# Many-head cross-attention: half of the bundles masked on GpSimd in SBUF, where matmuls masked them in PSUM

## The chip, the cores and the metric

The program runs on one core of one Trainium2 chip, in one launch. It is a whole network of twelve layers, each a stage of its own. The metric is the device time of the program in microseconds, the median over runs. Engines go by the profile's names: PE is TensorE (PEld its weight loads), DVE is VectorE, ACT is ScalarE, POOL is GpSimd, SP is SyncE, which issues the loads.

## The reference

Only the seventh layer is touched, `_L2_xattn_ref`: cross-attention with 16 heads of 8 dimensions, from 64 queries to 1601 keys, for each of 32 batch elements. The mask is the same for all elements and heads.

```python
def _L2_xattn_ref(query, key, value, mask, W_q, W_k, W_v, W_o):
    Q = _split(query @ W_q.T)          # (32, 16, 64, 8)
    K = _split(key @ W_k.T)            # (32, 16, 1601, 8); key = value = ctx_1024
    V = _split(value @ W_v.T)
    scores = jnp.einsum('bhqd,bhkd->bhqk', Q, K) / jnp.sqrt(jnp.float32(D_K))
    scores = jnp.where(mask, -jnp.inf, scores)
    attn_w = jax.nn.softmax(scores, axis=-1)
    attn_w = jnp.nan_to_num(attn_w, nan=0.0)
    out = jnp.einsum('bhqk,bhkd->bhqd', attn_w, V)
    ...
    return merged @ W_o.T
```

`query` is the layernorm of x, and the result is added to x.

## The kernel before

`many_head_cross_attention` (from line 2458) is one stage with five engine programs that meet at semaphores. Everything is in fp32, except for a few bf16 constants. The order of each engine's work is written out by hand over a common counter b, one step for one bundle.

**Bundles.** The keys of an element are cut into 13 chunks of 128 (the last has 65). A bundle is two chunks of keys by half of the heads (two groups of four, `gi` 0 and 1, which sit in two row groups of 32 of TensorE). Seven pairs of chunks (`step` 0 to 6, the last a single chunk) times two halves (`half` 0, even, and 1, odd) make `ROUND` = 14 bundles for an element and 448 in all.

**Steps of TensorE** at b, in order:
- `less_max(b)` writes minus the row's maximum into the score banks `st` (three, in turn, one for each `gi`; it waits until the exponentials have read the bank).
- `query_by_keys(b + LEAD)` makes scores in the other orientation, 18 bundles ahead, for the maxima (three banks `mx`).
- `no_bounds(b)`, line 2610, for even bundles only: up to eight bf16 matmuls which add 2 x -2^100 (`bounds`, made of the mask) to the masked scores through one-hot columns (`places_b`), so that their exponential is 0.
- `keys_by_query(b)`, line 2621, adds keys times queries.
- `values(b - 2)`, line 2670, multiplies the exponentials of an earlier bundle with the values and adds them up in the bank `pv`. For an even bundle it waits for the exponentials (`exped`), for an odd one for VectorE's cap (`capped`). The first bundle of an element is done three behind.
- `prepare`: one unit of a later element's transposes (T), values (V) or keys (K), through the bank `prep`, or of the ends (M, E1 to E3).

**The others.** ScalarE takes the exponential of both halves of a bundle into `pT[b % 5]` in SBUF (lines 2846 and 2849; it waits until the values of the bundle five back are done) and copies the prepared units. VectorE does the masked maxima of bundle b + 18 (line 2765: one pass each, scores in PSUM plus the mask in SBUF), and for odd bundles the cap, line 2811: a tensor_tensor minimum of the exponentials with `capT`, which is 0 for a masked key and 2 for an open one. An open exponential is near or below 1, so it passes. It also copies `pv` out and does the ends of an element. GpSimd has one instruction per element, the spread of the queries into `qb` (line 2583), which waits until the scores three elements back are done. SyncE loads weights, constants, the mask in several layouts and then the keys of each element.

Of the kernel before, what the change touches and what calls it, by code (L numbers as in the profile page):

```python
# [2457 lines left out]
def many_head_cross_attention(c, name):  # L2458
# [9 lines left out]
    with Stage(c, name) as s:  # L2468
# [14 lines left out]
        pT = [s.sb(f"pT{u}", [P, 2, 2, 256]) for u in range(5)]  # L2483
# [24 lines left out]
        capped = s.sem("capped")  # L2508
# [63 lines left out]
        def _(pool):  # L2572
# [4 lines left out]
            pool.wait_ge(loaded, 304)  # L2577
            for n in range(B):
                if n == 0:
                    pool.wait_ge(*V.at("q3"))  # L2580
# [4 lines left out]

        @block.tensor
        def _(pe):
# [3 lines left out]
            pe.wait_ge(loaded, 304)  # L2591
# [10 lines left out]

            def no_bounds(b, n, step, half, i, c2):

                j = 2 * step + c2
                if j >= KC:
                    return
                for gi in (0, 1):
                    w, r = 2 * b + gi, 32 * (2 * half + gi)
                    nc.tensor.matmul(st[0:chunk[j], w % 3, 256 * c2:256 * c2 + 256], bounds[i][r:r + 32, P * j:P * j + chunk[j]],  # L2610
                                     places_b[i][r:r + 32, :, :].rearrange("p h q -> p (h q)"), start=False, stop=False,
                                     tile_position=(r, 0))
# [40 lines left out]
            def values(b):  # L2653
# [4 lines left out]
                else:  # L2658
                    pe.wait_ge(exped, 2 * b + 2)
# [76 lines left out]
        def _(dve):  # L2736
            dve.wait_ge(loaded, 304)
# [60 lines left out]
            for b in range(FIRST, LAST):  # L2798
# [14 lines left out]
                n, off = divmod(b - ROUND - 1, ROUND)  # L2813
# [376 lines left out]
```

## Time and profile before

| what | value |
|---|---|
| median of 3 runs | 3734.1 us (3729.46 to 3734.45) |
| profiled execution, its time | 3733.86 us |
| its span | 3732.0 us, mean granted TensorE clock 0.848 |
| busy over the span | TensorE 2816.8 us (75%), VectorE 2138.5 (57%), ScalarE 1409.1 (38%), GpSimd 425.2 (11%) |
| this stage | from about 1173 to 2515 us of the span; its bundles from about 1288 to 2511 |

Busy times are those of each engine by itself, and an engine that waits isn't busy. Matmuls are pipelined and their ends are modelled, so that starts of instructions tell more than busy shares of TensorE. A row of the timeline has the start in us from the start of the span, the duration, engine, line, operation, output and inputs with their shapes, how many of them in a row, and in brackets how long the engine was idle before and what ended it. A mean in a group is in ns.

### The profile page before, as it was taken

Reading aid. Unit: us, or ns where it says so; the run is one execution under the profiler, and the core shown is the slowest. Engines: PE = TensorE matmul, PEld = TensorE weight load, DVE = VectorE, ACT = ScalarE, POOL = GpSimd, SP = SyncE. Lnnn points to the kernel's source line nnn. Section 1 sums busy time; section 2 is a strip of 40 time slices with the busy share of each in tenths; the row PEclk is TensorE's granted clock in tenths of the full one; section 3 lists DMA queues with packets and bytes.
Section 4 is the critical chain, followed back from the end, with each engine's and each line's share of the span. In section 5 each row is a group of like instructions: output and inputs, shape, how many; then the busy total and the mean of one; then the engine's idle time right before and its main releaser. Section 6 shows DMA issues by size and latency. Waiting matters only on the chain. (4 is left out here: it accounts for less than half of the span.)

```text
span 3732.0 us, 67368 instructions
## 1 busy us (share of the span) xinstructions
PE 2816.8 (75%) x27776; PEld 1805.1 (48%) x27806; DVE 2138.5 (57%) x6291; ACT 1409.1 (38%) x2463; POOL 425.2 (11%) x275
## 2 busy tenths in 40 slices
PE   7866743696986999999999999993544557887723
PEld 4655532464664466666666666651211224565412
DVE  4432312574112377777777777745999853444776
ACT  3431211463332255555555555533211122443521
POOL 2310011340000000000000000000445400001300
PEclk9995776797998599999999999976777767898956
DMA  7740032000001001010000101001122100552000
GB/s 168 176 104 0 14 96 50 7 3 13 18 18 29 27 20 28 20 28 20 28 20 20 28 20 28 2 6 50 68 112 90 45 12 9 134 133 53 8 0 11
DMA packets 207265, 160.11 MB, mean 43 GB/s; under 512 B 12194, under 2 KB 195717, under 8 KB 202832
## 3 DMA queue, kind: packets, MB, share of 16 engines
q1 hardware_dynamic: 205936, 153.95, 15.0%
q8 instruction: 221, 3.62, 0.4%
q0 software_dynamic: 1024, 1.85, 0.2%
q14 instruction: 84, 0.69, 0.1%
HBM read 151.57 MB, written 4.46 MB: 42 GB/s over the span
## 5 line engine op out<-in xcount | busy, mean ns | idle before, releaser
L2765 DVE CUSTOM_DVE_ANT_0 L_xattn_junk<-L_xattn_ps_mx,L_xattn_shift 128x512 f32<-128x512 f32 (+1 forms) x1024 | 545.0, 569 | 360.0 <-issue 358.9
L2846 ACT ACTIVATE L_xattn_pT<-L_xattn_ps_st 128x512 f32<-128x512 f32 x768 | 416.8, 595 | 421.1 <-PE L_xattn_ps_st L2621 421.1
L2634 PE MATMUL L_xattn_ps_mx<-L_xattn_kT,L_xattn_qb 32*128 32x512 f32 (+1 forms) x2048 | 501.8, 568 | 0.4 <-ACT L_xattn_kT L2861 0.4
L2621 PE MATMUL L_xattn_ps_st<-L_xattn_qb,L_xattn_kT 32*128 32x256 f32 (+1 forms) x3328 | 447.3, 383 | 0.0
L2621 PEld LDWEIGHTS L_xattn_ps_st<-L_xattn_qb,L_xattn_kT 32*128 32x128 f32 (+1 forms) x3328 | 297.0, 185 | 24.6
L2811 DVE TENSOR_TENSOR L_xattn_pT<-L_xattn_pT,L_xattn_capT 128x512 f32<-128x512 f32 (+1 forms) x448 | 271.4, 647 | 37.3 <-ACT L_xattn_pT L2846 32.4
L2670 PE MATMUL L_xattn_ps_pv<-L_xattn_pT,L_xattn_v 128*17 128x128 f32 x6656 | 268.0, 280 | 0.0
L2670 PEld LDWEIGHTS L_xattn_ps_pv<-L_xattn_pT,L_xattn_v 128*17 128x17 f32 x6656 | 148.0, 98 | 162.6 <-issue 161.1
L2634 PEld LDWEIGHTS L_xattn_ps_mx<-L_xattn_kT,L_xattn_qb 32*128 32x128 f32 x2048 | 161.7, 188 | 8.8 <-DVE L_xattn_tops L2765 6.1
L2044 ACT ACTIVATE L_attn_da<-L_attn_dt,L_attn_na 128x2016 f32<-128x2016 f32 x32 | 63.2, 1976 | 270.2 <-DVE L_attn_db L2003 140.2
L1785 DVE SCALAR_TENSOR_TENSOR x<-L_ffn_ps_o,L_ffn_weights,x 128x128 f32<-128x128 f32 x128 | 36.1, 345 | 224.5 <-PE L_ffn_ps_o L1698 224.5
L2583 POOL TENSOR_TENSOR L_xattn_qb<-ln_sq,L_xattn_four 128x256 f32<-128x256 f32 x32 | 19.5, 612 | 1198.3 <-PE L_xattn_ps_st L2621 1170.8
L447 PE MATMUL L_xattn_ps_turn<-ident,L_xattn_ctx 128*128 128x128 f32 (+1 forms) x832 | 126.3, 289 | 39.1 <-ACT L_xattn_ctxT L564 28.2
L2647 PE MATMUL L_xattn_ps_st<-L_xattn_less,L_xattn_ones_b 3*128 3x512 bf16 x768 | 154.8, 391 | 1.1 <-ACT L_xattn_pT L2846 1.1
L1932 PE MATMUL L_attn_ps_all<-L_attn_db,ident 128*128 128x512 f32 x128 | 84.4, 820 | 87.5 <-POOL L_attn_db L1955 87.5
L1816 ACT ACTIVATE L_ffn_gelu<-L_ffn_ps_h,L_ffn_b1e 128x512 f32<-128x512 f32 x128 | 87.8, 687 | 163.4 <-PE L_ffn_ps_h L1691 160.1
L1698 PE MATMUL L_ffn_ps_o<-L_ffn_w,L_ffn_gelu 128*128 128x128 f32 x1024 | 122.8, 278 | 24.9 <-ACT L_ffn_gelu L1816 24.9
L1698 PEld LDWEIGHTS L_ffn_ps_o<-L_ffn_w,L_ffn_gelu 128*128 128x128 f32 x1024 | 116.7, 192 | 51.4 <-ACT L_ffn_gelu L1816 51.4
L2692 PE MATMUL L_xattn_ps_prep<-L_xattn_wv,L_xattn_ctxT 128*128 128x128 f32 (+1 forms) x832 | 132.0, 300 | 2.3 <-ACT L_xattn_v L2864 2.0
L2610 PE MATMUL L_xattn_ps_st<-L_xattn_place_b,L_xattn_bounds 32*128 32x256 bf16 (+1 forms) x1664 | 131.1, 272 | 0.0
L2696 PE MATMUL L_xattn_ps_prep<-L_xattn_ctxT,L_xattn_wk 128*128 128x512 f32 (+1 forms) x256 | 128.2, 584 | 2.4 <-ACT L_xattn_kT L2861 2.0
L447 PEld LDWEIGHTS L_xattn_ps_turn<-ident,L_xattn_ctx 128*128 128x128 f32 (+1 forms) x832 | 95.1, 146 | 68.1 <-issue 24.8
(552 smaller groups left out, 5472.2 us busy)
## 6 DMA issues: line engine op xcount, KB each, us to landing
L_xattn_ctx<-in_ctx SPq DMA_DIRECT2D x96, 768.0 KB
L_attn_bb<-scratch_rows SPq DMA_DIRECT2D x16, 1024.0 KB, 4.8
L_attn_cc<-scratch_rows SPq DMA_DIRECT2D x16, 1024.0 KB, 6.9
L_xattn_mask<-in_mask_keys SPq DMA_DIRECT2D x32, 400.2 KB, 6.9
L_ffn_w<-in_L_ffn_w SPq DMA_DIRECT2D x32, 256.0 KB, 3.1
L_ffn_w<-in_L_ffn_W SPq DMA_DIRECT2D x16, 256.0 KB, 3.0
L_xattn_mask<-in_mask_pairs SPq DMA_DIRECT2D x32, 100.1 KB, 4.5
L_xattn_ctx<-in_ctx SPq DMA_DIRECT2D x96, 32.5 KB
```

Source lines behind the costliest of these rows:

```text
L447: last = nc.tensor.transpose(tp[g % 2][:, P * (j % 4):P * (j % 4) + k], ctx[0:k, u, b, j, :], c.ident[0:k, 0:k])
L1698: last = nc.tensor.matmul(po[:, i % 2, P * j:P * j + P], g[:, i % 2, k, P * j:P * j + P], w2[:, u, k, :], start=(k == 0), stop=(k == FC - 1))
L2610: nc.tensor.matmul(st[0:chunk[j], w % 3, 256 * c2:256 * c2 + 256], bounds[i][r:r + 32, P * j:P * j + chunk[j]], places_b[i][r:r + 32, :, : ...
L2621: last = nc.tensor.matmul(st[0:chunk[j], w % 3, 256 * c2:256 * c2 + 256], kT[n % 3][r:r + 32, P * j:P * j + chunk[j]], qb[n % 3][r:r + 32, ...
L2634: last = nc.tensor.matmul(mx[:, w % 3, to:to + width], qb[n % 3][32 * g:32 * g + 32, 2 * (p % 2):2 * (p % 2) + 2, :].rearrange("p h q -> p ...
L2647: nc.tensor.matmul(st[:, w % 3, :], ones_b[r:r + 3, :], less[n % 2][r:r + 3, :, :].rearrange("p c k -> p (c k)"), start=True, stop=False, ...
L2670: last = nc.tensor.matmul(pv[32 * q:32 * q + 17, P * half:P * half + P], v[n % 3][0:chunk[j], j, 4 * half + q, :], pT[b % 5][0:chunk[j], c ...
L2692: last = nc.tensor.matmul(prep[0:chunk[j], to:to + P], ctxT[:, P * j:P * j + chunk[j]], wv[:, :], start=True, stop=True)
L2696: last = nc.tensor.matmul(prep[:, 0:width], wk[:, :], ctxT[:, 512 * m:512 * m + width], start=True, stop=True)
L2765: last = nc.vector.tensor_tensor_reduce(out=junk[:, w % 3, to:to + width], in0=mx[:, w % 3, to:to + width], in1=shift[:, k0:k0 + width], s ...
L2811: nc.vector.tensor_tensor(x, x, capT[0:k, j[0]:j[1], :].unsqueeze(2).broadcast_to([k, j[1] - j[0], 4, S]), ALU.min)\
L2846: nc.scalar.activation(pT[b % 5][:, :, gi, :], st[:, w % 3, :].rearrange("p (c k) -> p c k", c=2), ACT.Exp)\
```

## The change

The even bundles get no matmuls for the mask any more. Their exponentials are unmasked, as those of the odd ones, and GpSimd masks them in SBUF: for each `gi` a tensor_scalar (minimum with 2, then times 0.5), and then a tensor_tensor product with `capT` (0 or 2). The first bounds what may have overflowed, and the two factors cancel. GpSimd waits for `exped` ahead of each tensor_scalar, and for its own `clamped` ahead of each product; TensorE's `values` wait for `kept`. Values run three bundles behind (the first of an element four), `pT` has `HELD` = 7 buffers in place of five, and VectorE's copy of `pv` comes one bundle later. `bounds`, `places` and `masks` go, with their ten load issues at the start (`loaded` is awaited at 144 in place of 304) and the four VectorE instructions that made bf16 of them. The spreads of the first three elements are made up front, and that of element n + 2 behind bundle 14n + 2 in GpSimd's queue.

```diff
+    HELD = 7
...
-        pT = [s.sb(f"pT{u}", [P, 2, 2, 256]) for u in range(5)]
+        pT = [s.sb(f"pT{u}", [P, 2, 2, 256]) for u in range(HELD)]
...
-            return [x for x in (b - 3,) if x % ROUND == 0 and 0 <= x < BUNDLES] + \
-                [x for x in (b - 2,) if x % ROUND and 0 <= x < BUNDLES]
+            return [x for x in (b - 4,) if x % ROUND == 0 and 0 <= x < BUNDLES] + \
+                [x for x in (b - 3,) if x % ROUND and 0 <= x < BUNDLES]
...
-            for i in (0, 1):
-                sp.dma_start(places[i][:, :], a["c_thirty_two"][i]).then_inc(loaded, 16)
-                for g in range(GROUPS):
-                    sp.dma_start(masks[i][32 * g:32 * g + 32, :], a["mask_all"][32 * i:32 * i + 32, :]).then_inc(loaded, 16)
...
+            def keep(b, n, step, half):
+
+                k, j = (P, (2 * step, 2 * step + 2)) if step < 6 else (KREST, (KC - 1, KC))
+                x = [pT[b % HELD][0:k, 0:j[1] - j[0], gi, :].rearrange("p c (h q) -> p c h q", q=S) for gi in (0, 1)]
+                for gi in (0, 1):
+                    pool.wait_ge(exped, 2 * b + gi + 1)
+                    nc.gpsimd.tensor_scalar(x[gi], x[gi], 2.0, 0.5, ALU.min, ALU.mult).then_inc(clamped, 1)
+                for gi in (0, 1):
+                    pool.wait_ge(clamped, b + gi + 1)
+                    nc.gpsimd.tensor_tensor(x[gi], x[gi], capT[0:k, j[0]:j[1], :].unsqueeze(2).broadcast_to([k, j[1] - j[0], 4, S]), ALU.mult)\
+                        .then_inc(kept, 1)
+
+            pool.wait_ge(*V.at("q3"))
+            for n in range(3):
+                own_queries(n)
+            pool.wait_ge(*A.at("capT"))
+            for b in range(BUNDLES):
+                n, step, half = of_bundle(b)
+                if half == 0:
+                    keep(b, n, step, half)
+                if b % ROUND == 2 and 3 <= n + 2 < B:
+                    own_queries(n + 2)
...
-            def no_bounds(b, n, step, half, i, c2):
...
                 if half:
                     pe.wait_ge(capped, b + 1)
                 else:
-                    pe.wait_ge(exped, 2 * b + 2)
+                    pe.wait_ge(kept, b + 2)
...
-                    for i in (0, 1) if now[2] == 0 else ():
-                        no_bounds(b, *now, i, 0)
-                        no_bounds(b, *now, i, 1)
...
-            for i in (0, 1):
-                nc.vector.tensor_scalar(bounds[i][:, :], masks[i][:, :], 2 * OUT, None, ALU.mult)
-                nc.vector.tensor_copy(places_b[i][:, :, :], places[i][:, :].unsqueeze(1).broadcast_to([P, 4, S]))
...
-                n, off = divmod(b - ROUND - 1, ROUND)
+                n, off = divmod(b - ROUND - 2, ROUND)
...
-                    if b >= 5 and gi == 0:
-                        act.wait_ge(pv_done, b - 4)
+                    if b >= HELD and gi == 0:
+                        act.wait_ge(pv_done, b - HELD + 1)
```

## Rows read from the trace of the kernel before

**Rows 1.** Busy times of the stretch from 1364.87 us: us, engines (instructions), clock, DMA, GB/s.

```profile
...
1364.87:2395.08 1030.21, 1002.40 (x13836) 648.52 (x13828) 747.11 (x3376) 560.51 (x1108) 16.52 (x27) 1.00 0.08 23
```

**Rows 2.** Timeline of GpSimd in the stage: start us, us, what [idle before].

```profile
...
1364.87 0.61 POOL L2583 TENSOR_TENSOR L_xattn_qb<-ln_sq,L_xattn_four 128x256 f32<-128x256 f32 x1 [37.44 <-PE L_xattn_ps_st L2621]
...
1822.68 0.61 POOL L2583 TENSOR_TENSOR L_xattn_qb<-ln_sq,L_xattn_four 128x256 f32<-128x256 f32 x1 [37.44 <-PE L_xattn_ps_st L2621]
...
2395.08 0.61 POOL L2583 TENSOR_TENSOR L_xattn_qb<-ln_sq,L_xattn_four 128x256 f32<-128x256 f32 x1 [37.64 <-PE L_xattn_ps_st L2621]
```

**Rows 3.** Timeline of TensorE's weight loads: the first of three steps.

```profile
...
1799.30 0.09 PEld L2647 LDWEIGHTS L_xattn_ps_st<-L_xattn_less,L_xattn_ones_b 3*128 3x128 bf16 x2 [0.76 <-ACT L_xattn_pT L2846]
...
1802.10 0.09 PEld L2647 LDWEIGHTS L_xattn_ps_st<-L_xattn_less,L_xattn_ones_b 3*128 3x128 bf16 x2 [0.76 <-ACT L_xattn_pT L2846]
...
1805.34 0.09 PEld L2647 LDWEIGHTS L_xattn_ps_st<-L_xattn_less,L_xattn_ones_b 3*128 3x128 bf16 x2 [0.76 <-ACT L_xattn_pT L2846]
```

**Rows 4.** Groups of instructions from 1200 to 2500 us: busy us, mean ns | idle before.

```profile
...
L2811 DVE TENSOR_TENSOR L_xattn_pT<-L_xattn_pT,L_xattn_capT 128x512 f32<-128x512 f32 x444 | 269.4, 648 | 27.6 <-ACT L_xattn_pT L2846 25.9 <-ACT L_xattn_pT L2849 1.6
...
L2610 PE MATMUL L_xattn_ps_st<-L_xattn_place_b,L_xattn_bounds 32*128 32x256 bf16 x1660 | 130.5, 271 | 0.0
```

**Rows 5.** Groups of GpSimd over the whole span, by shape.

```profile
...
L405 POOL TENSOR_SCALAR L_xattn_out_keys<-L_xattn_mask 128x1601 f32<-128x1601 int32 x16 | 68.1, 4256 | 0.1
...
L403 POOL COPY L_xattn_qk<-xn 128x128 f32<-128x128 f32 x32 | 9.3, 291 | 577.5 <-ACT xn L556 248.4 <-PE L_xattn_ps_scores L494 191.1 <-ACT L_xattn_shift L585 128.7
L770 POOL TENSOR_TENSOR L_attn_qT<-L_attn_straight_q,L_attn_turned_q 128x512 f32<-128x512 f32 x4 | 5.1, 1270 | 6.0 <-DVE L_attn_turned_q L865 6.0
```

**Rows 6.** Timeline of VectorE and GpSimd about 696 us, another stage.

```profile
694.35 0.16 DVE L182 SCALAR_TENSOR_TENSOR ln_shift<-ln_mean_var,ln_rstd 128x4 f32<-128x4 f32 x1
694.43 0.60 DVE L185 TENSOR_SCALAR xn<-x,ln_mean_var,ln_rstd 128x128 f32<-128x128 f32 x2
...
696.39 0.66 DVE L185 TENSOR_SCALAR xn<-x,ln_mean_var,ln_rstd 128x128 f32<-128x128 f32 x2
696.42 0.55 POOL L995 TENSOR_SCALAR L_attn_bp<-L_attn_bp 128x128 f32<-128x128 f32 x1 [5.32 <-DMA L_attn_shift<-in_c_shift]
696.93 0.60 POOL L1001 COPY L_attn_v<-xn 128x512 f32<-128x512 f32 x1
...
697.17 0.38 DVE L182 SCALAR_TENSOR_TENSOR ln_shift<-ln_mean_var,ln_rstd 128x4 f32<-128x4 f32 x1
```

**Rows 7.** Timeline of VectorE and GpSimd in the state-space stage.

```profile
2623.09 2.27 DVE L2000 TENSOR_TENSOR L_attn_db<-L_attn_xi,L_attn_bb 128x2048 f32<-128x2048 f32 x1
2623.32 6.38 POOL L1955 TENSOR_TENSOR L_attn_db<-L_attn_db,L_attn_cc 128x2048 f32<-128x2048 f32 x1 [227.63 <-DVE L_attn_db L2003]
2625.39 8.60 DVE L2003 TENSOR_TENSOR_SCAN L_attn_db<-L_attn_da,L_attn_db 128x2048 f32<-128x2048 f32 x1
2634.07 4.51 POOL L1955 TENSOR_TENSOR L_attn_db<-L_attn_db,L_attn_cc 128x2048 f32<-128x2048 f32 x1 [4.36 <-DVE L_attn_db L2003]
2634.12 6.61 DVE L2000 TENSOR_TENSOR ln_sq<-L_attn_xi,L_attn_bb 128x2048 f32<-128x2048 f32 x1
2640.76 4.42 DVE L2003 TENSOR_TENSOR_SCAN ln_sq<-L_attn_da,ln_sq 128x2048 f32<-128x2048 f32 x1
```

**Rows 8.** Timeline of VectorE about the query spread of 1822.68 us.

```profile
...
1822.52 0.69 DVE L2765 CUSTOM_DVE_ANT_0 L_xattn_junk<-L_xattn_ps_mx,L_xattn_shift 128x512 f32<-128x512 f32 x1 [0.90 <-issue]
```

**Rows 9.** Timeline of SyncE's issues and of VectorE where the stage begins.

```profile
1176.06 1.15 SPq L2558 DMA_DIRECT2D L_xattn_mask<-in_mask_all  x2
...
1182.08 0.43 SPq L2567 DMA_DIRECT2D L_xattn_ctx<-in_ctx  x1
...
1183.51 0.99 DVE L2738 TENSOR_SCALAR L_xattn_shift<-L_xattn_mask 128x1601 f32<-128x1601 uint8 x1 [10.93 <-DMA L_xattn_mask<-in_mask_all]
...
1185.32 0.99 DVE L2741 TENSOR_SCALAR L_xattn_bounds<-L_xattn_mask 128x1601 bf16<-128x1601 uint8 x1
...
1187.58 0.11 DVE L2743 MEMSET L_xattn_zero_b<- 128x64 uint32 x1
```

More of the change, by code:

```diff
@@ L2473, in many_head_cross_attention @@
         cap, capT = s.sb("cap", [P, KEYS]), s.sb("capT", [P, KC, S])
-        masks = [s.sb(f"mask{i}", [P, KEYS], U8) for i in (0, 1)]
-        bounds = [s.sb(f"bounds{i}", [P, KEYS], BF16) for i in (0, 1)]
-        places, places_b = [s.sb(f"place{i}", [P, S]) for i in (0, 1)], [s.sb(f"place_b{i}", [P, 4, S], BF16) for i in (0, 1)]
         ones_b = s.sb("ones_b", [P, P], BF16)
@@ L2507, in many_head_cross_attention @@
         chain = s.sem("chain")
-        capped = s.sem("capped")
+        capped, clamped, kept = s.sem("capped"), s.sem("clamped"), s.sem("kept")
         def early(b):
@@ L2576, in _, with own_queries @@
             nc.gpsimd.memset(parts[:, :, :, :], 0.0).then_inc(filled, 1)
[L2577 to L2580, printed above, removed]
+            pool.wait_ge(loaded, 144)
+            def own_queries(n):
                 if n >= 3:
@@ L2590, in _ @@
             pe.wait_ge(*A.at("ln_T3"))
-            pe.wait_ge(loaded, 304)
+            pe.wait_ge(loaded, 144)
             for i in range(4):
@@ L2601, in _ @@
             pe.wait_ge(*A.at("capT"))
-            def no_bounds(b, n, step, half, i, c2):
[L2605 to L2612, printed above, removed]
             def keys_by_query(b, n, step, half, c2):
@@ L2670, in values @@
                         last = nc.tensor.matmul(pv[32 * q:32 * q + 17, P * half:P * half + P], v[n % 3][0:chunk[j], j, 4 * half + q, :],
-                                                pT[b % 5][0:chunk[j], c2, q // 2, P * (q % 2):P * (q % 2) + P],
+                                                pT[b % HELD][0:chunk[j], c2, q // 2, P * (q % 2):P * (q % 2) + P],
                                                 start=False, stop=(j == KC - 1 and half == 1), tile_position=(0, 32 * q))
@@ L2736, in _ @@
         def _(dve):
[L2737 removed]
+            dve.wait_ge(loaded, 144)
             nc.vector.tensor_scalar(shift[:, :], mask[:, :], OUT, None, ALU.mult)
             nc.vector.tensor_scalar(cap[:, :], mask[:, :], -2.0, 2.0, ALU.mult, ALU.add)
[L2740 to L2742 removed]
             nc.vector.memset(zero_b[:, :], 0.0).then_inc(V.did("set"), 1)
@@ L2808, in _ @@
                         k, j = (P, (2 * step, 2 * step + 2)) if step < 6 else (KREST, (KC - 1, KC))
-                        x = pT[b % 5][0:k, 0:j[1] - j[0], gi, :].rearrange("p c (h q) -> p c h q", q=S)
+                        x = pT[b % HELD][0:k, 0:j[1] - j[0], gi, :].rearrange("p c (h q) -> p c h q", q=S)
                         dve.wait_ge(exped, 2 * b + gi + 1)
@@ L2842, in exps @@
                     act.wait_ge(scored, w + 1)
-                    if b >= 5 and gi == 0:
-                        act.wait_ge(pv_done, b - 4)
+                    if b >= HELD and gi == 0:
+                        act.wait_ge(pv_done, b - HELD + 1)
                     if step < 6:
-                        nc.scalar.activation(pT[b % 5][:, :, gi, :], st[:, w % 3, :].rearrange("p (c k) -> p c k", c=2), ACT.Exp)\
+                        nc.scalar.activation(pT[b % HELD][:, :, gi, :], st[:, w % 3, :].rearrange("p (c k) -> p c k", c=2), ACT.Exp)\
                             .then_inc(exped, 1)
                     else:
-                        nc.scalar.activation(pT[b % 5][0:KREST, 0, gi, :], st[0:KREST, w % 3, 0:256], ACT.Exp).then_inc(exped, 1)
+                        nc.scalar.activation(pT[b % HELD][0:KREST, 0, gi, :], st[0:KREST, w % 3, 0:256], ACT.Exp).then_inc(exped, 1)
             def taken(unit):
```

## The prediction

> **What bounds the kernel now.** I read the page first, for its busy slices, where one long stretch stands out with TensorE nearly full: the loop of this stage. Next the busy times by stretch. From 1364.87 to 2395.08 us [rows 1], TensorE is busy 1002.4 of 1030.2 us at a granted clock of 1.00 (the 2.4 GHz level), VectorE 747.1, ScalarE 560.5, GpSimd 16.5. So the order of TensorE's queue sets the pace, and GpSimd is nearly empty. The timeline of GpSimd gives the period: its only instruction in the loop comes once a batch element, at 1364.87 and, 27 elements later, at 2395.08 [rows 2], so one element (14 bundles) takes 1030.21 / 27 = 38.16 us, and 32 of them 1221 us. A busy share of 97% could be a modelled one, so I then took TensorE's steps by the start of their first weight load [rows 3]: they follow without a gap that another engine explains. TensorE is the bound, and what leaves its queue is time, as long as nobody else becomes slower than what is left.
>
> **What TensorE loses.** The mask matmuls (line 2610) are 1664 in number; the group shows 130.5 us of busy time for the 1660 in its window [rows 4]. That overstates them: matmuls of the two row groups overlap. The steps say it better. Two neighbouring steps with the same preparation work are 1799.30 to 1802.10 (odd bundle, no mask matmuls, 2.80 us) and 1802.10 to 1805.34 (even bundle, eight of them, 3.24 us) [rows 3]. The eight cost 0.44 us. Per batch element there are six such even bundles and one with four: 6 x 0.44 + 0.22 = 2.86 us. TensorE alone could then do an element in 35.3 us; over 32 elements that is 91.5 us less.
>
> **What GpSimd gains.** For each of the seven even bundles of an element: two tensor_scalar (minimum, then times 0.5) and two tensor_tensor products, six times on 128x512 and once on 65x256. The prices:
> - The product. Nearest is the tensor_tensor with two separate inputs of 128x512: 1.27 us [rows 5]. The query spread of this stage (128x256, both inputs repeated) takes 0.61 [rows 2]; with a fixed part of 0.19 (from the copies: 0.291 us for 128 elements, 0.60 for 512 [rows 5, 6], so 0.8 ns an element) it is 1.64 ns an element, or 1.03 us for 512. The score operand isn't repeated, so I take 1.27, and 0.73 for 256 elements (the same slope).
> - The tensor_scalar. No row has it at 128x512 in fp32. There are two: 128x128 in fp32 took 0.55 us [rows 6], and 128x1601 from int32 took 4.25 [rows 5]. With the fixed 0.19 they give 2.8 and 2.5 ns an element. Was the 0.55 only a wait? VectorE ran two small tensor_scalars beside it; the pair took 0.66 us against 0.60 elsewhere, and the second was not held up to the end of GpSimd's instruction [rows 6]. So I take it as GpSimd's own. Two rows of different size and type on one line give 0.19 + 512 x 2.54 = 1.49, or 1.63 by the steeper slope: I take 1.50, and 0.84 for 256 elements. The low bounds are 0.86 (0.55, then the copy's 0.8 ns for the other 384 elements: the extra is a fixed one) and 0.60 (as fast as a copy).
>
> GpSimd's own work per element is 6 x (2 x 1.27 + 2 x 1.50) = 33.2, plus 2 x 0.73 + 2 x 0.84 = 3.1 for the small bundle, plus the spread at 0.61: 37.0 us. Consecutive ones overlap by 0.04 (0.55 from 696.42 runs to 696.97, the next starts at 696.93 [rows 6]); 29 of them give back 1.2. That alone is above TensorE's 35.3.
>
> **The shared access.** The timeline of the state-space stage shows how VectorE and GpSimd get on. A GpSimd product started at 2634.07 takes 4.51 us; VectorE's tensor_tensor started at 2634.12 takes 6.61 instead of 2.27, that is until GpSimd is done plus its own time. The other way round, GpSimd's product at 2623.32, begun 0.23 us behind a VectorE tensor_tensor, takes 6.38 instead of 4.51, and VectorE's next instruction, at 2625.39, takes 8.60 instead of 4.42, for GpSimd, already waiting, went first [rows 7]. A GpSimd copy does it too: VectorE's 0.16 us scalar_tensor_tensor at 697.17 took 0.38, up to the end of the copy at 697.53 [rows 6]. So a VectorE instruction with two SBUF inputs and GpSimd's work exclude each other. In this stage those are the caps of the odd bundles (line 2811, 0.648 us [rows 4]): twelve of 128x512 and two small ones per element. The masked maxima, with one input in PSUM, are not: the spread at 1822.68 takes its usual 0.61 with one of them running through it in its usual 0.69 [rows 2, 8]. A cap holds GpSimd for 2.10 / 2.27 of its streaming time (from the stretch of 1.87 plus the 0.23 lead), about 0.50 us, the small one 0.25: 12 x 0.50 + 2 x 0.25 = 6.5 us per element.
>
> **The sum.** GpSimd per element: 37.0 - 1.2 + 6.5 = 42.3 us. VectorE's own work is 747.1 / 27 = 27.7; its caps now wait, the first for about half a GpSimd instruction (0.7), the second for a whole one (1.4), some 2.1 for each of 6.5 pairs, so 41.4: just below. TensorE has 35.3 and waits: in values(b) for `kept`, with the preparation matmuls and the next bundle's scores queued behind it. The seven buffers don't shorten that, they only let it settle. So the stage goes at 42.3 an element, 4.14 more than now, over 32 elements +132.5 us.
>
> Ahead of the loop: ten DMA issues go, and the first key load moves from 1182.08 to where the needed loads end, 1177.21, so VectorE's start (1183.51, it waits for the mask load) comes some 4.5 us earlier; its bound and place instructions, 1185.32 to 1187.58, go too [rows 9]. All of it is in front of the layernorm and hidden by nothing: -6.8. Values one bundle later at the very end: +0.5. Moving the queries' spread ahead costs nothing, it is needed eight bundles later. The next stages don't change. Against the profiled execution's 3733.9 us (its span 3732.0, the median of the runs 3734.1): 3733.9 + 132.5 - 6.8 + 0.5 = **3860 us**.
>
> **A rule that speaks the other way.** The rows above put the tensor_scalar at three times a copy. The Trainium skill (GPSIMD Engine Reference, section Engine selection) says that one-input work on GpSimd runs at roughly line rate and only two-input work about half as fast as VectorE. By that rule the tensor_scalar would be a copy's equal, and the outcome that of the first rival; the trace agrees for the copies and not for either tensor_scalar row.
>
> **The rivals.**
> 1. *The tensor_scalar is cheap* (0.60 to 0.96). GpSimd's element is 13 tensor_scalars' worth (twelve and two halves, t each, plus 0.2), 16.7 for the products, 0.6 for the spread and 5.3 for caps less overlap. With t = 0.86 that is 34.0, below TensorE's 35.3, and TensorE stays the bound: 3733.9 - 91.5 - 6.3 = 3636, up to 3680 if the caps' waits are felt. TensorE overtakes GpSimd at t = 0.96. For it: only two rows, one with a type conversion and one of 128 elements, price the instruction. Against: they lie on one line. Chance 0.27.
> 2. *In between* (t from 0.96 to 1.20): 3680 to 3734; the point of no gain is t = 1.20, where 13 x 1.20 + 0.2 + 16.7 + 0.6 + 5.3 = 38.4. Chance 0.06, half of it within 0.2% of before (about what a measurement of this kernel can tell from no change).
> 3. *VectorE and GpSimd lock each other out in turn.* At 41.4 and 42.3 they are so near that each late cap delays the maxima, these TensorE, and this the exponentials that GpSimd wants: 2 to 3 us more per element, 3925 to 3960. The same comes out if two operations in one tensor_scalar cost more than the one of the rows (1.7 us: 13 x 0.2 = 2.6 us per element). Chance 0.15.
> 4. *The forecast*: 0.52. Its own range is 3825 to 3920 (t from 1.42 to 1.63, caps fully or half in series).
>
> Faster therefore 0.27 + 0.03 = 0.30, the same 0.03, slower 0.67. The range for 8 in 10 must reach into the first rival and into the third: 3645 to 3935.
>
> **What the changed profile should show.** 896 new GpSimd instructions, 1.5 us for a 128x512 tensor_scalar and 1.27 for a product, more where a cap ran first; GpSimd busy above 95% of the loop; the spread every 42.3 us; caps at a mean well above 0.65, up to 2; maxima still 0.69; TensorE near 83% busy with waits for the product (the `kept` wait) ahead of the values; the stage's first instruction after the mask load some 4.5 us earlier. If the spread comes every 35.3 us and GpSimd is idle a few per cent, the tensor_scalar's price was wrong and the first rival holds. If the tensor_scalar takes 1.5 and the period is above 44, it is the third. What would refute the scheme itself is a cap running beside a GpSimd product with neither stretched.

## The result: 3951 us in place of 3733, and the profile after

The changed kernel takes 3951.1 us (3932.5 to 3956.1, four runs), the kernel before 3732.6: a ratio of 1.058, 95% interval 1.055 to 1.061. The forecast was 3860, the range ended at 3935. The profiled execution took 3950.5 us (its span 3948.4).

The loop first: the stretch from one spread of the queries to another, 28 elements later, answers to [rows 1].

```profile
core 0: us, PE busy (x) PEld busy (x) DVE busy (x) ACT busy (x) POOL busy (x), PEclk, DMA share, GB/s
1340.69:2606.90 1266.21, 1119.06 (x12904) 664.42 (x12896) 1038.98 (x3513) 580.67 (x1151) 1233.35 (x814) 0.90 0.07 18
```

The spreads themselves, from the timeline of GpSimd [rows 2]:

```profile
1340.69 0.61 POOL L2577 TENSOR_TENSOR L_xattn_qb<-ln_sq,L_xattn_four 128x256 f32<-128x256 f32 x1
...
2606.90 0.60 POOL L2577 TENSOR_TENSOR L_xattn_qb<-ln_sq,L_xattn_four 128x256 f32<-128x256 f32 x1
```

1266.21 / 28 = 45.2 us an element, where it was 38.16. GpSimd is busy 97% of it, TensorE 88%, and the granted clock is 0.90, no longer 1.00. So GpSimd sets the pace, as forecast, at 45.2 and not 42.3. These 2.9 us, 32 times, make 93 us; 91 were missed. The prices, from the groups by shape, 1200 to 2700 us:

```profile
L2586 POOL TENSOR_SCALAR L_xattn_pT<-L_xattn_pT 128x512 f32<-128x512 f32 x379 | 762.9, 2028 | 115.1 <-ACT L_xattn_pT L2846 114.9
L2589 POOL TENSOR_TENSOR L_xattn_pT<-L_xattn_pT,L_xattn_capT 128x512 f32<-128x512 f32 x378 | 503.4, 1350 | 0.0
L2765 DVE CUSTOM_DVE_ANT_0 L_xattn_junk<-L_xattn_ps_mx,L_xattn_shift 128x512 f32<-128x512 f32 x768 | 500.6, 684 | 277.7 <-issue 276.3
L2811 DVE TENSOR_TENSOR L_xattn_pT<-L_xattn_pT,L_xattn_capT 128x512 f32<-128x512 f32 x378 | 476.8, 1302 | 19.2 <-ACT L_xattn_pT L2846 19.2
...
L2586 POOL TENSOR_SCALAR L_xattn_pT<-L_xattn_pT 65x256 f32<-65x256 f32 x62 | 65.7, 1076 | 4.0 <-ACT L_xattn_pT L2849 4.0
```

The tensor_scalar takes 2.03 us where 1.50 was forecast; the product 1.35 (1.27); the maxima are untouched at 0.68. The full caps doubled, from 0.69 us to 1.30 (the 0.65 of [rows 4] is a mean that mixes in the small ones).

How caps and GpSimd meet, from the timelines of both engines. First a cap that costs nothing: it starts 0.76 us into the second of two tensor_scalars (at 1464.61), takes its usual 0.69, and the two take 3.79, which is their usual time too. (The second cap of this pair, 0.6 us later, is one of those that are held: it takes 3.57.)

```profile
1462.73 3.79 POOL L2586 TENSOR_SCALAR L_xattn_pT<-L_xattn_pT 128x512 f32<-128x512 f32 x2
...
1465.37 0.69 DVE L2811 TENSOR_TENSOR L_xattn_pT<-L_xattn_pT,L_xattn_capT 128x512 f32<-128x512 f32 x1
```

Then the worst kind. Two caps that start at 1833.28 take 5.96 us: the first is held from the middle of a tensor_scalar through two products and the spread, for 4.5 us. TensorE's scores for the maxima then wait 3.27 us for VectorE.

```profile
1829.97 4.24 POOL L2586 TENSOR_SCALAR L_xattn_pT<-L_xattn_pT 128x512 f32<-128x512 f32 x2
1834.17 2.50 POOL L2589 TENSOR_TENSOR L_xattn_pT<-L_xattn_pT,L_xattn_capT 128x512 f32<-128x512 f32 x2
1836.63 0.61 POOL L2577 TENSOR_TENSOR L_xattn_qb<-ln_sq,L_xattn_four 128x256 f32<-128x256 f32 x1
...
1833.28 5.96 DVE L2811 TENSOR_TENSOR L_xattn_pT<-L_xattn_pT,L_xattn_capT 128x512 f32<-128x512 f32 x2
...
1839.90 0.28 PEld L2640 LDWEIGHTS L_xattn_ps_mx<-L_xattn_kT,L_xattn_qb 32*128 32x128 f32 x1 [3.27 <-DVE L_xattn_tops L2765]
```

The windows show TensorE's clock right behind that wait at its lower level, 1.2 GHz:

```profile
1840.00:1842.00 2.00, 2.00 (x14) 1.17 (x18) 1.09 (x5) 0.00 (x0) 2.00 (x2) 0.50 0.00 0
```

Of 318 full caps from 1400 to 2600 us, 162 took under 0.70 us, 33 above 3.5; their mean is 1.32.

Ahead of the loop, SyncE's mask load and VectorE's first instructions [rows 9]:

```profile
1174.08 1.14 SPq L2556 DMA_DIRECT2D L_xattn_mask<-in_mask_all  x2
...
1177.41 1.00 DVE L2741 TENSOR_SCALAR L_xattn_shift<-L_xattn_mask 128x1601 f32<-128x1601 uint8 x1 [6.82 <-DMA L_xattn_mask<-in_mask_all]
...
1179.30 0.81 DVE L170 BATCH_NORM_STATS2 ln_stats<-x 128x6 f32<-128x128 f32 x4
```

VectorE had waited 10.93 us for the mask, now 6.82: 4.1 less; with the four instructions that went (2.3) that is 6.4. The forecast had 6.8 for it.

### The profile page after: what moved, and what is told of

Same layout as the page of the kernel before. It is cut to its first block and busy times, and to the rows that moved or that the text cites. A ratio compares the mean times of both kernels' runs of the same rounds, so it can differ in the third digit from the quotient of the medians.

```text
span 3948.4 us, 64951 instructions
## 1 busy us (share of the span) xinstructions
PE 2907.4 (74%) x26142; PEld 1795.9 (45%) x26142; DVE 2421.6 (61%) x6287; ACT 1407.1 (36%) x2463; POOL 1811.6 (46%) x1171
## 5 line engine op out<-in xcount | busy, mean ns | idle before, releaser
L2586 POOL TENSOR_SCALAR L_xattn_pT<-L_xattn_pT 128x512 f32<-128x512 f32 (+1 forms) x448 | 840.5, 1891 | 120.3 <-ACT L_xattn_pT L2846 116.1
L2640 PE MATMUL L_xattn_ps_mx<-L_xattn_kT,L_xattn_qb 32*128 32x512 f32 (+1 forms) x2048 | 587.4, 616 | 35.0 <-DVE L_xattn_tops L2765 34.5
L2589 POOL TENSOR_TENSOR L_xattn_pT<-L_xattn_pT,L_xattn_capT 128x512 f32<-128x512 f32 (+1 forms) x448 | 559.5, 1267 | 0.0
L2811 DVE TENSOR_TENSOR L_xattn_pT<-L_xattn_pT,L_xattn_capT 128x512 f32<-128x512 f32 (+1 forms) x448 | 519.8, 1200 | 34.2 <-ACT L_xattn_pT L2846 29.3
L2627 PE MATMUL L_xattn_ps_st<-L_xattn_qb,L_xattn_kT 32*128 32x256 f32 (+1 forms) x3328 | 514.1, 424 | 0.0
L2627 PEld LDWEIGHTS L_xattn_ps_st<-L_xattn_qb,L_xattn_kT 32*128 32x128 f32 (+1 forms) x3328 | 344.9, 204 | 25.0
L2676 PE MATMUL L_xattn_ps_pv<-L_xattn_pT,L_xattn_v 128*17 128x128 f32 x6656 | 300.8, 306 | 63.8 <-POOL L_xattn_pT L2589 63.6
L2640 PEld LDWEIGHTS L_xattn_ps_mx<-L_xattn_kT,L_xattn_qb 32*128 32x128 f32 x2048 | 186.9, 205 | 70.6 <-DVE L_xattn_tops L2765 67.6
L2653 PE MATMUL L_xattn_ps_st<-L_xattn_less,L_xattn_ones_b 3*128 3x512 bf16 x768 | 177.1, 425 | 2.2 <-ACT L_xattn_pT L2846 1.4
L1955 POOL TENSOR_TENSOR L_attn_db<-L_attn_db,L_attn_cc 128x2048 f32<-128x2048 f32 x16 | 87.2, 5452 | 196.7 <-DVE L_attn_db L2003 196.7
```

The source lines that it names most:

```text
L2586: nc.gpsimd.tensor_scalar(x[gi], x[gi], 2.0, 0.5, ALU.min, ALU.mult).then_inc(clamped, 1)
L2589: nc.gpsimd.tensor_tensor(x[gi], x[gi], capT[0:k, j[0]:j[1], :].unsqueeze(2).broadcast_to([k, j[1] - j[0], 4, S]), ALU.mult)\
L2627: last = nc.tensor.matmul(st[0:chunk[j], w % 3, 256 * c2:256 * c2 + 256], kT[n % 3][r:r + 32, P * j:P * j + chunk[j]], qb[n % 3][r:r + 32, ...
L2640: last = nc.tensor.matmul(mx[:, w % 3, to:to + width], qb[n % 3][32 * g:32 * g + 32, 2 * (p % 2):2 * (p % 2) + 2, :].rearrange("p h q -> p ...
L2653: nc.tensor.matmul(st[:, w % 3, :], ones_b[r:r + 3, :], less[n % 2][r:r + 3, :, :].rearrange("p c k -> p (c k)"), start=True, stop=False, ...
L2811: nc.vector.tensor_tensor(x, x, capT[0:k, j[0]:j[1], :].unsqueeze(2).broadcast_to([k, j[1] - j[0], 4, S]), ALU.min)\
```

## The experiments

Theory: GpSimd's sum sets the pace, and its tensor_scalar was priced too low. Rivals: VectorE and GpSimd lock each other out; or TensorE's own saving wasn't there. "Period" is the time per element between spreads, 28 elements.

**1. Even bundles without a mask.**

```diff
-                if half == 0:
-                    keep(b, n, step, half)
...
-                    pe.wait_ge(kept, b + 2)
+                    pe.wait_ge(exped, 2 * b + 2)
```

> The changed kernel, where the even bundles aren't masked at all (no matmuls, nothing on GpSimd; their exponentials go into the values as they are, so the output lacks the mask there). It prices what left TensorE's queue. By the sum of the prediction: 35.3 us an element, 3733.9 - 91.5 - 6.3 = 3636 us. Rival: ScalarE's or VectorE's order holds the steps up as soon as they are shorter; then the element takes 36 to 37.5 us and the time is 3660 to 3705.

One run: 3665.5 us, period 36.38, clock 1.00 in the loop. That is the rival's range. What left TensorE's queue is worth 1.8 us an element in this order, not 2.9.

**2. The product alone.**

```diff
-                    nc.gpsimd.tensor_scalar(x[gi], x[gi], 2.0, 0.5, ALU.min, ALU.mult).then_inc(clamped, 1)
-                for gi in (0, 1):
-                    pool.wait_ge(clamped, b + gi + 1)
```

> The changed kernel without the tensor_scalar of GpSimd: only the product with capT is left for the even bundles (so they aren't bounded, and count twice). GpSimd's own work falls from 41.4 to about 17 us an element. If the work of GpSimd sets the pace of the changed kernel, TensorE becomes the bound again: 3636 to 3660 us. If the exclusion between VectorE's caps and any GpSimd work is what costs, the time stays well above: with 14 products in the place of 28 instructions the caps still wait some 0.6 us each, 8 us of VectorE time an element, 3690 or more.

One run: 3683.8 us, period 36.87, clock 1.00, between the two ranges. GpSimd is busy 17.3 us of it. The products cost 0.5 us an element over experiment 1; all else that the change loses needs the tensor_scalar. This doesn't price a cap held by a product: here only 28 of 392 products overlapped a cap at all, and no cap took more than its usual time.

**3. One operation in the tensor_scalar.**

```diff
-                    nc.gpsimd.tensor_scalar(x[gi], x[gi], 2.0, 0.5, ALU.min, ALU.mult).then_inc(clamped, 1)
+                    nc.gpsimd.tensor_scalar(x[gi], x[gi], 2.0, None, ALU.min).then_inc(clamped, 1)
```

> The changed kernel with a tensor_scalar of one operation (minimum with 2) in place of two (minimum, then times 0.5), so that the even bundles count twice. Theory A, the price goes by the number of operations: 0.19 + (1.90 - 0.19) / 2 = 1.05 us, 11 us less an element, TensorE is the bound at 35.3 us or a little more, 3640 to 3690 us. Theory B, the price goes by elements, and the rows of before (2.5 ns an element) were of one operation: 1.5 us, 13 x 0.4 = 5.2 us less an element than 45.2, so 40 us, 3785 us.

One run: 3855.1 us, period 42.11, of it GpSimd idle 2.7. An undisturbed tensor_scalar takes 1.49 us, the price of theory B, but the time is 70 us above its sum: with caps beside it the mean is 1.60, a product's 1.44, and GpSimd waits.

**4. Without VectorE's caps of the odd bundles.**

```diff
-                    pe.wait_ge(capped, b + 1)
+                    pe.wait_ge(exped, 2 * b + 2)
...
-                        nc.vector.tensor_tensor(x, x, capT[0:k, j[0]:j[1], :].unsqueeze(2).broadcast_to([k, j[1] - j[0], 4, S]), ALU.min)\
-                            .then_inc(capped, 1)
```

> The changed kernel without VectorE's caps on the odd bundles (they stay unmasked; TensorE waits for the exponentials alone). GpSimd's work is as in the changed kernel. If GpSimd's own instructions set the pace, the element comes down from 45.2 us to their sum without stretches and idle time, 41.4 to 42 us: 32 x 3.5 = 112 less, 3840 us. If the wait for each other was the larger part (the prediction had 6.5 us of it an element, and a third rival with more), the element goes under 39 us, 3750 us or less.

One run: 3876.0 us, period 43.13, GpSimd busy 41.45 of it: the sum as expected, and 1.7 us of idle time on top of it, with no cap in the kernel. Its groups show the undisturbed prices:

```profile
L2586 POOL TENSOR_SCALAR L_xattn_pT<-L_xattn_pT 128x512 f32<-128x512 f32 x278 | 529.0, 1921 | 15.8 <-ACT L_xattn_pT L2837 15.5
L2589 POOL TENSOR_TENSOR L_xattn_pT<-L_xattn_pT,L_xattn_capT 128x512 f32<-128x512 f32 x280 | 349.8, 1272 | 0.0
```

So two operations cost 1.92 us, and all that the caps add to the changed kernel is 45.2 - 43.1 = 2.1 us an element: 2.6 more of busy time, 0.5 less of idle time. TensorE waits for GpSimd here (from 1400 to 2500 us; us in total, times, longest), and its granted clock in the loop is 0.91:

```profile
PEld L_xattn_ps_pv L2676 <- POOL L_xattn_pT L2589: 114.9, 94, 2.1
```

**5. One operation, and no caps.** Both edits together.

> The changed kernel with the minimum alone in the tensor_scalar (the factor 0.5 cancels in the normalisation) and without VectorE's caps of the odd bundles (their mask is left out). GpSimd's own work is then 12 x (1.48 + 1.27) + 3.1 + 0.6 - 1.2 = 35.5 us an element. With caps the same kernel took 42.1, 2.7 of it idle. Theory (the caps and what follows from them, late maxima and exponentials, are the whole of the difference): 36.4 to 37.2 us, 3665 to 3695 us, clock 1.00 in the stage. Rival: GpSimd's idle time comes from TensorE and ScalarE handing over exponentials late whatever VectorE does: 38.5 us or more, above 3735 us.

One run: 3698.8 us, period 37.19, as the theory had it (the clock is 0.985, not 1.00). The tensor_scalar is 1.49 us. The same kernel with caps took 42.1: here the caps cost 4.9 us, more than twice as much as where GpSimd is slower. In the one with caps, GpSimd's instructions and VectorE's small product in the ends of an element read:

```profile
L2586 POOL TENSOR_SCALAR L_xattn_pT<-L_xattn_pT 128x512 f32<-128x512 f32 x287 | 453.6, 1596 | 34.6 <-ACT L_xattn_pT L2846 34.6
L2589 POOL TENSOR_TENSOR L_xattn_pT<-L_xattn_pT,L_xattn_capT 128x512 f32<-128x512 f32 x286 | 407.2, 1444 | 0.0
...
L2792 DVE TENSOR_TENSOR L_xattn_coef<-L_xattn_vinv,L_xattn_own_dims 128x128 f32<-128x128 f32 x24 | 32.8, 1366 | 0.8
```

That last product (0.29 us elsewhere) is waited for by TensorE; experiment 10 shows what this does.

**6. The order alone**: the kernel before, with values three behind, seven buffers and the copy of `pv` one bundle later (the main lines of the edit).

```diff
-            return [x for x in (b - 3,) if x % ROUND == 0 and 0 <= x < BUNDLES] + \
-                [x for x in (b - 2,) if x % ROUND and 0 <= x < BUNDLES]
+            return [x for x in (b - 4,) if x % ROUND == 0 and 0 <= x < BUNDLES] + \
+                [x for x in (b - 3,) if x % ROUND and 0 <= x < BUNDLES]
```

> The kernel before with its mask matmuls, its masks and its loads, and of the change only the order: values three bundles behind (four for the first of an element), seven buffers of exponentials, the copy of the value sums one bundle later. Theory: the order costs nothing but one bundle at the very end, about +0.5 us, so 3733 to 3736 us and a period of 38.15 us. Rival: the later values cost TensorE time themselves (another order of its queue against ScalarE's copies), and are what is missing of the saving on TensorE (36.4 us an element measured without a mask on the even bundles, 35.3 forecast): then a period of 38.5 to 39.2 and 3745 to 3770 us.

3742.7 us, ratio to the kernel before 1.0028 (95% interval 1.0016 to 1.0039), period 38.54. The theory falls: the order costs 0.39 us an element.

**7. All caps on VectorE**, nothing masked by GpSimd.

```diff
+    ON_POOL = ()
...
-                if half == 0:
+                if on_pool(b):
                     keep(b, n, step, half)
...
-                if now and now[2]:
+                if now and not on_pool(b):
```

`on_pool(b)` is true for the even bundles whose step is in `ON_POOL`; experiments 8 to 10 change this one line, and the waits count accordingly.

> Nothing on GpSimd: VectorE caps the even bundles as it does the odd ones, one minimum of 0.65 us for each of the two halves. Theory (the mask matmuls' room is real, GpSimd was the wrong place): VectorE goes from 27.7 to 27.7 + 8.5 = 36.2 us of busy time an element, TensorE's floor is the 36.4 measured without masks, and the two so near make 36.8 to 37.8 us a period, 3685 to 3717 us, with VectorE over 95% busy. Rival: VectorE, which also does the maxima 18 bundles ahead in the same queue, becomes the bound as GpSimd did, late maxima stop TensorE and the clock falls: 38.3 us or more, 3735 to 3800.

3703.6 us, ratio 0.991 (0.988 to 0.993), period 37.27: 0.9% faster than before, as the theory had it.

**8. Three of the seven even bundles on GpSimd**, the other four on VectorE (bundles 0, 4 and 8 of 14).

> GpSimd masks three of the seven even bundles of an element (steps 0, 2 and 4), VectorE caps the other four with its one minimum. Theory (the number of GpSimd instructions decides, the scheme itself is sound): GpSimd has 3 x 6.4 + 0.6 = 19.8 us an element, VectorE 27.7 + 3 x 1.3 + 0.7 = 32.3, TensorE's floor of 36.4 decides: 36.4 to 37.0 us, 3665 to 3688 us. Rival: each pair of instructions that shares the access makes a cap late by up to 4 us, and late maxima are what costs, not GpSimd's sum: 37.8 us or more, above 3715 us.

3823.1 us, ratio 1.024 (1.023 to 1.026), period 40.88, and GpSimd idle for 19.9 us of it. The theory falls, and with it the idea that only a full GpSimd costs. TensorE waits in every element 1.0 us for maxima and about 2.0 for the addition to x (1.4 in experiment 7), and the loop's clock is 0.96.

**9. Two**, bundles 4 and 6.

> As the kernel with three even bundles on GpSimd, but with two, steps 2 and 3 (bundles 4 and 6 of 14), VectorE caps the other five. The three cost 4.0 us an element above the products alone; by the steps of the exponentials 2.1 us of them lie behind bundle 0's masks, 1.4 behind bundle 8's, where VectorE has the ends of the last element and the negated maxima, and none behind bundle 4's. Theory (it is the place: a cap that is late by 1 to 2 us costs only where TensorE has no slack, and then stops it and halves its clock): none of the two is in such a place, 36.9 to 37.4 us an element, 3685 to 3710 us. Rival (any two-operation tensor_scalar beside a cap costs, 1.3 us a bundle): 39 us or more, above 3755.

3767.3 us, ratio 1.009 (1.008 to 1.011), period 39.60, and GpSimd idle for 25.5. These are the rival's numbers (39 us or more, above 3755): by these two kernels each mask costs some 1.2 us, wherever it is. One mask at a time tells the two accounts apart.

**10. One**, bundle 4 or bundle 6.

> GpSimd masks one even bundle an element, bundle 4 of 14; VectorE caps the other six. Nothing else differs from the kernel with all caps on VectorE (37.27 us an element, 3703.6 us). Theory (place): bundle 4's mask meets only caps and maxima, with slack behind both, so the steps of the exponentials stay as with all caps on VectorE: 37.0 to 37.4, 3695 to 3708 us, clock 1.00 in the stage. Rival (each mask costs, 1.2 us each by the kernels with three and with two): 38.4 to 38.6 us, 3740 to 3750 us.

> The same with bundle 6. Its mask begins 0.8 us earlier than in the kernel with two, where it had to wait for bundle 4's, and lasts some 6.3 us; its last product then ends some 2.4 us behind bundle 8's exponential in place of 3.1, and VectorE's small product for the ends of the element starts there or just before. Theory (place): either that product escapes, then 37.0 to 37.4 us and 3695 to 3708, or it is held for up to 0.6 us and TensorE's wait for it halves the clock: one wait at the steps after bundles 8 and 9, up to 39.5 us and 3765. Rival (each mask costs): 38.4 to 38.6 as with bundle 4, spread over other steps.

Bundle 4: 3718.7 us, ratio 0.995 (0.994 to 0.997), period 37.64. Bundle 6: 3800.4 us, ratio 1.017 (1.015 to 1.019), period 40.62. The rival falls: it wanted 38.4 to 38.6 us of both. The theory of the place holds, though both are above its ranges: 3.4 us an element for one place and 0.4 for the other, by the same four instructions. Below, the mean time from the first exponential of a bundle to that of the next, over 25 elements; the last column is their sum. It differs a little from the period where the elements vary.

```
bundle             0    1    2    3    4    5    6    7    8    9   10   11   12   13    sum
before          2.62 3.06 2.27 2.99 2.80 3.24 2.80 3.34 2.11 2.55 2.47 3.41 2.18 2.31  38.15
order alone     2.84 3.06 2.62 2.18 3.44 3.24 2.80 3.34 2.11 2.55 2.47 3.41 2.18 2.31  38.54
unmasked even   2.80 2.62 2.62 1.93 3.25 2.80 2.80 2.90 2.17 2.11 2.88 3.38 2.21 1.91  36.38
all on VectorE  2.80 2.62 2.62 2.03 3.28 2.80 2.80 2.90 2.17 2.11 3.63 3.38 2.21 1.91  37.27
bundle 4        2.80 2.62 2.62 2.03 3.28 2.80 2.80 2.90 2.54 2.11 3.64 3.38 2.21 1.91  37.64
bundle 6        2.80 2.62 2.62 2.03 3.28 2.80 2.80 2.90 4.72 3.84 2.73 3.41 2.21 1.91  40.67
three           2.80 2.62 2.77 3.19 4.09 2.80 2.80 2.90 2.40 2.11 4.70 3.55 2.21 1.91  40.87
changed kernel  2.85 2.60 3.96 2.33 4.97 3.46 2.92 3.55 3.24 3.82 3.42 3.61 2.21 2.24  45.18
```

With bundle 6, all of it lies behind bundles 8 and 9 (+2.6 and +1.7; bundle 10 gives 0.9 back). The timelines of GpSimd, VectorE and TensorE's weight loads there:

```profile
1866.60 3.81 POOL L2595 TENSOR_SCALAR L_xattn_pT<-L_xattn_pT 128x512 f32<-128x512 f32 x2 [18.04 <-ACT L_xattn_pT L2855]
1870.38 2.94 POOL L2598 TENSOR_TENSOR L_xattn_pT<-L_xattn_pT,L_xattn_capT 128x512 f32<-128x512 f32 x2
...
1869.84 2.36 DVE L2820 TENSOR_TENSOR L_xattn_pT<-L_xattn_pT,L_xattn_capT 128x512 f32<-128x512 f32 x2
...
1872.55 0.92 DVE L2801 TENSOR_TENSOR L_xattn_coef<-L_xattn_vinv,L_xattn_own_dims 128x128 f32<-128x128 f32 x1
1873.50 0.29 DVE L2804 TENSOR_TENSOR L_xattn_own<-L_xattn_ps_prep,L_xattn_coef 128x128 f32<-128x128 f32 x1
...
1873.85 0.50 PEld L2721 LDWEIGHTS L_xattn_ps_prep<-L_xattn_delta,L_xattn_own 128*128 128x128 f32 x2 [1.98 <-DVE L_xattn_own L2804]
```

GpSimd's products held the second of two caps (the pair took 2.36 us for 1.29) and the small product behind them (0.92 for 0.29, until the mask ended), together 1.7 us, and TensorE waited 1.98. Then comes its clock. The windows about that wait:

```profile
1870.00:1872.00 2.00, 2.00 (x36) 1.34 (x36) 2.00 (x2) 0.38 (x1) 2.00 (x3) 1.00 0.04 8
...
1875.00:1877.00 2.00, 2.00 (x24) 1.22 (x22) 1.89 (x18) 0.18 (x1) 0.00 (x0) 0.50 0.00 0
1877.00:1879.00 2.00, 2.00 (x24) 1.22 (x20) 1.87 (x8) 0.91 (x2) 0.00 (x0) 0.50 0.00 0
...
1873.70:1880.40 6.70, 6.55 (x52) 4.21 (x52) 5.34 (x39) 1.09 (x2) 0.00 (x0) 0.50 0.00 1
1880.60:1882.60 2.00, 2.00 (x36) 1.52 (x34) 2.00 (x7) 1.67 (x3) 0.00 (x0) 1.00 0.00 0
```

At 2.4 GHz ahead of the wait, it runs at 1.2 GHz for 6.7 us and more. TensorE's busy time an element rises from 35.1 us (experiment 7) to 37.9 by this alone, for its work is the same: 2.8 of the 3.4 us. The length of the wait isn't all that counts. With two masks, a wait of 1.40 at the same place brought the loop's clock down to 0.93; with all caps on VectorE, one of 1.35 at another step comes in every element and leaves it at 1.00:

```profile
1900.84 0.30 PEld L2721 LDWEIGHTS L_xattn_ps_prep<-L_xattn_delta,L_xattn_own 128*128 128x128 f32 x2 [1.40 <-DVE L_xattn_own L2804]
```

```profile
1873.10 0.42 PEld L2702 LDWEIGHTS L_xattn_ps_prep<-ident,L_xattn_ctx 128*128 128x128 f32 x4 [1.35 <-DVE x L2836]
...
1321.86:2365.29 1043.43, 982.75 (x12888) 605.72 (x12881) 986.95 (x3893) 578.08 (x1149) 17.14 (x29) 1.00 0.08 23
```

With bundle 4 the mask ended before these ends, and the small product took its usual time:

```profile
1827.65 3.44 POOL L2598 TENSOR_TENSOR L_xattn_pT<-L_xattn_pT,L_xattn_capT 128x512 f32<-128x512 f32 x2
...
1835.19 0.29 DVE L2801 TENSOR_TENSOR L_xattn_coef<-L_xattn_vinv,L_xattn_own_dims 128x128 f32<-128x128 f32 x1
```

**11. GpSimd's instructions in another order**, in the changed kernel: each product behind its own tensor_scalar.

```diff
                     nc.gpsimd.tensor_scalar(x[gi], x[gi], 2.0, 0.5, ALU.min, ALU.mult).then_inc(clamped, 1)
-                for gi in (0, 1):
                     pool.wait_ge(clamped, b + gi + 1)
```

> The changed kernel with GpSimd's four instructions of a bundle in another order: tensor_scalar and product of the first half, then both of the second. GpSimd's sum stays. In the changed kernel a cap could be held from a second tensor_scalar through two products, the spread and the next start, 4.5 us. Theory (late caps are what idles GpSimd 1.2 us an element and stretches it by 2.6): behind each product now comes a tensor_scalar with its free 1.4 us, no cap is held above about 2.5 us, and the period falls from 45.2 to 42.8 to 44.0, less 0.1 for each product that now waits for the end of the instruction just ahead (1.4 an element more): 3890 to 3940 us. Rival: the order doesn't matter, GpSimd's sum alone counts: 45.2 to 46.6, 3950 to 3995 us.

One run: 3948.4 us, period 45.67. Half of the theory holds: no cap took over 1.78 us, their mean fell from 1.32 to 1.00, and TensorE no longer waits for maxima (2.1 us an element in the changed kernel). But the time didn't follow, and the period is the rival's. GpSimd stayed busy for 44.5 us of a period; the other 1.17 are gaps under 0.1 us between its instructions, it never waits for exponentials. TensorE waits for GpSimd instead, and its clock is 0.87. In the changed kernel late caps aren't the bound, GpSimd's own sum and its stretch are.

**12. All caps on VectorE, values two behind** and five buffers, the order of before.

> The kernel before without mask matmuls, masks, bounds and places, and with VectorE's cap for every bundle. Values two bundles behind, five buffers, as before. Theory: the later values cost 0.39 us an element (measured with the order alone), and VectorE's caps come early enough for two behind: 37.27 - 0.39 = 36.9, that is 3685 to 3698 us. Rival: the caps of even bundles come too late for values two behind, TensorE waits for each: 37.8 or more, 3715 us or above.

3675.0 us, ratio 0.985 (0.983 to 0.987), period 36.74: the fastest kernel of the study that computes the whole reference, and a little better than expected (0.53 us an element below three behind, not 0.39).

**13. The same, with the addition to x ahead of that step's caps** in VectorE's queue.

> As the kernel with all caps on VectorE and values two behind, and VectorE adds the element's result to x (a bank that TensorE's next transposes wait for) ahead of that step's caps, not behind them. With all caps on VectorE and values three behind, the step after bundle 10 took 3.63 us, 2.88 without those caps, with TensorE waiting 1.35 us for this addition. Theory: 0.6 to 0.75 of it come back, 36.1 to 36.4 us an element, 3660 to 3680 us. Rival: the addition then waits for TensorE's product in VectorE's queue and holds caps and maxima behind it: no gain, 3690 us or above.

3680.7 us, ratio 0.987 (0.985 to 0.988), period 36.72: no gain over experiment 12, the rival's outcome in part. The addition doesn't wait for TensorE in VectorE's queue, as the rival had it, but the maxima behind it are late. TensorE's weight loads at the step behind bundle 10, first of 12, then of 13:

```profile
1717.10 0.42 PEld L2666 LDWEIGHTS L_xattn_ps_prep<-ident,L_xattn_ctx 128*128 128x128 f32 x4 [1.34 <-DVE x L2800]
```

```profile
1712.03 0.42 PEld L2666 LDWEIGHTS L_xattn_ps_prep<-ident,L_xattn_ctx 128*128 128x128 f32 x4 [0.21 <-DVE x L2782]
...
1713.79 0.18 PEld L2616 LDWEIGHTS L_xattn_ps_mx<-L_xattn_kT,L_xattn_qb 32*128 32x128 f32 x1 [0.86 <-DVE L_xattn_tops L2738]
```

The wait for the addition is gone, and one for the maxima, now behind the same work of VectorE, stands in its place: VectorE's queue is what is late there, in both orders.

## Why the forecast fell short, point by point

1. **The tensor_scalar at 1.50 us ("I take 1.50, and 0.84 for 256 elements"): the step that failed.** The estimate from the two rows of [rows 5, 6] was right for what it was made from, instructions with one operation (both are, in the kernel's source): 1.49 us (experiment 5). The kernel's has two, and takes 1.92. The second operation costs 0.43 us. Per element 12 x 0.42 + 2 x 0.22 = 5.5 us. The prediction had this case as half of its third rival, at 1.7 us, and its chance of 0.15 was too small: no row had two operations at all, and the 1.7 rests on no row either.
2. **"A cap holds GpSimd for ... 6.5 us per element": too high.** GpSimd's busy time is 41.45 us an element without caps and 44.05 with them, a stretch of 2.6. About half of the caps start where a tensor_scalar lets them through (162 of 318 took their usual time); the rows of [rows 7], on which the term rests, were all products. The caps' own worst case was put too low: up to 2 us forecast, up to 4.5 measured. The Trainium skill (SBUF — State Buffer, section SBUF: two separate sides) says that of a GpSimd instruction and a VectorE one with two SBUF inputs the one that starts first has the shared ports for the whole instruction. For a cap met by a product the traces agree (in experiment 10 the held cap ends 0.55 us behind the product's end). Beside a tensor_scalar they do not: caps that start 0.6 us or more into it take their usual 0.69, in 141 of 181 cases in the changed kernel and in all 351 of experiments 3 and 8 to 11.
3. **GpSimd's idle time was put at nothing; it is 1.2 us.** It waits for exponentials. That looks like the third rival's chain (late caps, late maxima, TensorE stopped and then at the lower clock), and TensorE does wait 2.1 us an element for maxima. But the chain isn't shown to be the cause: without any cap, and with no wait for maxima left, GpSimd idles 1.7 us for exponentials (experiment 4). There TensorE waits for GpSimd's products and its clock falls. What makes the exponentials late in the changed kernel stays open.
4. **The sum**: 42.3 + 5.5 - 3.9 + 1.2 = 45.1, measured 45.2. That the forecast came within 91 us is in part luck: the caps' term, too high by 3.9, hid most of the 5.5 that the tensor_scalar's lacked.
5. **TensorE's floor of 35.3 was too low**, 36.4 by experiment 1, which would have mattered in the first rival only. The later values cost 0.39 (experiment 6), and of the 2.86 for the mask matmuls 38.54 - 36.38 = 2.16 came back: the table has its 0.44 at bundles 1, 5, 7 and 9, but bundles 10 and 11, where waits decide, give nothing or lose.
6. **Right**: GpSimd as the bound, the direction, 1.27 for the product, the maxima untouched, and the setup within half a microsecond. That "the seven buffers don't shorten that" wasn't tested by itself.
7. **The rule on one-input work**, weighed in the prediction: the Trainium skill (GPSIMD Engine Reference, section Engine selection) puts it roughly at line rate, which here would be a copy's 0.60 us [rows 6]. Measured with one operation it is 1.49, with two 1.92: the rule fails for this instruction, which takes 2.5 and 3.2 times the copy.

Experiments 8 to 10 show a cost that the forecast didn't see, and that remains where GpSimd has time to spare: masks on GpSimd lose against VectorE's caps even where GpSimd is nearly idle. The condition, shown in the traces of experiment 10, is that they meet a VectorE instruction with two SBUF inputs that TensorE soon waits for. Whether this also holds for each late step of the changed kernel itself wasn't separated; its excess in the table over the kernel with unmasked even bundles lies mostly at bundles 2, 4, 8 and 9. What stays open: why a cap that starts 1.0 to 1.5 us into a second tensor_scalar was let through in some cases and held for over 3.5 us in 33, and why this happened in the changed kernel alone.

## What to carry to other kernels

Price an instruction from a row with the same number of operations, not only the same operands; where there is none, let the range reach as far as the second operation may cost as much as the first. A partly idle engine isn't a free one: before work is moved onto GpSimd, look in VectorE's queue for two-input SBUF instructions that TensorE waits for, since here a wait of 2 us cost 3.4. And try first whether the engine that already does half of a job can do all of it: VectorE, at 28 of 38 us, took the other caps and made the kernel 1.5% faster.

## What the runs showed of the hardware

- GpSimd's tensor_scalar on 128x512 fp32: 1.49 us with one operation, 1.92 with two, beside 1.27 for a tensor_tensor product and 0.60 for a copy. On 65x256: 0.84 and 1.06, the product 0.73.
- A tensor_scalar mostly excludes VectorE's two-input instruction only at its start. A cap that began 0.11 us into one took 1.04 us, one that began at 0.37 took 0.78; less the usual 0.69, each was free at some 0.47 us of the 1.9. Of those that began from 0.6 us on, 351 of 351 took the usual time in experiments 3 and 8 to 11, but in the changed kernel only 141 of 181. A product holds a cap to its end.
- Back-to-back GpSimd instructions can pass a waiting cap: two products and the spread did, for 4.5 us. With the two kinds in turn the longest was 1.78.
- One wait of TensorE of 2 us, in a loop at the 2.4 GHz level, was followed by some 6.7 us at 1.2 GHz, and made the element 3.4 us longer. A wait of 1.35 us at another step, in every element, left the clock at 1.00.
